# Softplus from ScalarE's table in a four-layer state-space model with a mixture of experts

## The chip, the cores and the metric

The kernel runs on one core of a Trainium2 chip. The metric is the device time of one execution in microseconds (us), the median of some runs. The engines of the core work side by side, each through its own list of instructions in order, and wait for each other on semaphores: TensorE (PE in the profile, PEld its weight loads), VectorE (DVE), ScalarE (ACT), GpSimd (POOL), and the queue of SyncE (SP), which issues most of the DMAs.

## What is computed

4096 tokens (16 sequences of 256) of width 128 go through four layers of a state-space block, then a residual and a layer norm, then a mixture of 8 experts (the best 2 of them per token) with residual and layer norm. Everything is in fp32. The block, cut to what matters here:

```python
def _mamba_block(x, p):
    xn = _rmsnorm(x, p['norm_w'])
    xp, z = jnp.split(xn @ p['Win'], 2, axis=-1)
    xc = silu(conv(xp, p['conv_w'], p['conv_b']))
    dt, Bm, Cm = jnp.split(xc @ p['Wx'], [64, 80], axis=-1)
    delta = jax.nn.softplus(dt @ p['Wdt'] + p['bdt'])
    A = -jnp.exp(p['A_log'])
    # per token t: h = exp(delta_t * A) * h + (delta_t * xc_t) * B_t ;  y_t = h . C_t
    y = (scan(xc, delta, A, Bm, Cm) + xc * p['Dp']) * silu(z)
    return x + y @ p['Wblk']
```

The inner width is 256, the state has 16 entries per channel. softplus(v) is log(1 + exp(v)).

## The kernel before, in words

**Steps and windows.** The tokens are cut into 8 groups of 512 (two sequences); four layers times 8 groups make 32 steps. Every engine's code is written as a function `window(s, ...)` of 16 slots, in which step s is scanned while step s + 1 is prepared and step s - 1 is finished. `windows` calls it for s = -1 (prologue), 0 and 1, then in a hardware loop over pairs for s = 2 to 29, then for 30, 31 and 32. The expert stage behind it has 8 groups in the same form (`group_pairs`: two written out, two turns of a loop over pairs, two written out).

**A scan slot.** A slot scans two units of 32 channels by 4 state entries. ScalarE makes the decays exp(delta * A) of a slot from `d_rep` (L563, two of 510 columns) into a ring of 4; GpSimd and ScalarE make the products du * B (`outer`, L469 and L472, L641), one quarter m of the state for all channels in four slots; TensorE turns them to channels (`to_channels`, L1067); VectorE scans (L829); VectorE and GpSimd multiply by C in turn (`times_c`, L838 and L478); TensorE sums (L1052).

**Preparing step s + 1.** On ScalarE, in order: slot 3 the silus of xc and z (`silus`, L574 and L579), with a table load before and one after; slot 5 the copy of dt, B and C (L587); slot 6 the root of the norm of step s + 2; slots 7 and 8 softplus; slot 10 the copy of B (L617); slot 14 the copies of du turned to tokens (`copy_dut`, L626, into `du_t`). Between them stand the decays and products of every slot. TensorE feeds these through two banks, `pre_ps`: taps, z (`project_z`, L1090, at slot 2), dt (L1108), the turns of B and du (L1145, at slot 11). GpSimd multiplies delta by xc to du at slot 10 (L488). At slot 12 GpSimd's list has `outer` of the next step's first quarter with no product in it, only the waits for `du_t` and B, and behind it the multiplication by C of slot 11.

**Softplus.** It is computed as max(v, 0) + log(1 + exp(-|v|)), the logarithm bounded from above by a short polynomial. ScalarE: Abs and Relu of both 512-column halves out of PSUM with the bias dt (L600, L601), then Exp (L605), Square (L608) and Ln (L610) over all 1024 columns. VectorE, at slot 8: two fused operations and an addition (L860, L864, L868), which give `delta` and release du and the copies of delta. All seven activations have their functions in the table set that the decays use, so no table is loaded for them.

**Queues.** SP issues in order for each window: the rows of C (`c_rep`), in even windows the output weights (`w_out`, after the output projection of the step before), then 16 copies of delta into `d_rep` (L357), which the decays of the next window read. In even windows ScalarE issues the load of the next weights (`w_pre`) right behind the Ln (L654), in odd windows a smaller one at slot 12. Instructions come to the engines by DMA as well (queues named instruction in the profile).

Of the kernel before, what the change touches and what calls it, by code (L numbers as in the profile page):

```python
# [10 lines left out]
ALU = mybir.AluOpType  # L11
# [5 lines left out]
EXPERTS, HID = 8, 512  # L17
# [22 lines left out]
LOG_SCALE = 3.0 ** -0.5  # L40
LOG_BIAS = -0.75 * LOG_SCALE
LOG_ADD = 13.0 / 16.0
LN_ERROR = 2.0 ** -23
# [22 lines left out]
def build_program(nc, xT, x_rows, norm_w, Win, conv_w, conv_b, Wx, Wdt, bdt, A_log, Dp, Wblk, Wout, bout,  # L66
                  gate_w, w1, w2, out):
    ctx = ExitStack()
    with ctx:
# [3 lines left out]
        def sem(name):  # L73
# [13 lines left out]
        sp_e = sb("sp_e", [128, KT, TG])  # L87
        sp_w = sb("sp_w", [128, KT, TG])
        sp_l = sb("sp_l", [128, KT, TG])
        delta = sb("delta", [128, KT, TG])  # L90
        du = sp_l
# [10 lines left out]
        one = sb("one", [128, 1])  # L102
        log_bias = sb("log_bias", [128, 1])
# [7 lines left out]
            sp_l[:, 0, JT * EXPERTS * i:JT * EXPERTS * (i + 1)].rearrange("p (j e) -> p j e", j=JT)  # L111
# [59 lines left out]
        x_in = [sp_e[:, i, :] for i in range(2)]  # L171
        x_fin = sp_w[:, 0, :]
        res1 = sp_w[:, 1, :]
# [41 lines left out]
        dt_used = sem("dt_used")  # L215
# [3 lines left out]
        act_sp = sem("act_sp")  # L219
        sp_ready = sem("sp_ready")  # L220
        dve_sp = sem("dve_sp")
# [54 lines left out]
        def wait(eng, semaphore, value):  # L276

            if isinstance(value, int) and value <= 0:
                return
            eng.wait_ge(semaphore, value)  # L280
# [25 lines left out]
        def has(s, offset):  # L306

            return not isinstance(s, int) or 0 <= s + offset < STEPS

        def group_pairs(eng, stage_fn):  # L310

            for par in (0, 1):
                stage_fn(par, 0, par)
            with eng.Fori(1, GROUPS // 2 - 1) as i:
                for par in (0, 1):
                    stage_fn(2 * i + par, i, par)
            for par in (0, 1):
                stage_fn(GROUPS - 2 + par, GROUPS // 2 - 1, par)
# [5 lines left out]
        def _(sp):  # L324
# [42 lines left out]
            def window(s, i, par):  # L367
                nxt = 1 - par
                if is_last(s):
                    sp.wait_ge(delta_ready, STEPS)  # L370
# [37 lines left out]
            windows(sp, window)  # L408
# [14 lines left out]
            group_pairs(sp, finish)  # L423
# [932 lines left out]
```

## Time and profile before

| | |
|---|---|
| median of 3 runs | 2142.69 us (2141.18 to 2149.81) |
| profiled execution, span | 2143.5 us |
| VectorE busy | 1943.2 us (91%) |
| TensorE busy | 1877.8 us (88%) |
| ScalarE busy | 1683.8 us (79%) |
| GpSimd busy | 1458.1 us (68%) |
| scan loop and its ends | to about 1710 us |
| expert stage | from about 1710 us to the end |

For the profiled execution the profile gives its span, from the first instruction to the last, and no other time; it lies 0.8 us above the median. In the expert stage TensorE is busy without a break and GpSimd has nothing to do, so the shares of the whole span say little of the scan. Times within the span are counted from its start. A row of a timeline has the start, the length, engine, line, operation, what it writes and reads, how many in a row were merged, and in brackets how long the engine stood idle before and for whom.

### The profile page before, as it was taken

To read this page: it belongs to the slowest core of one execution; us is meant where nothing else is said; L and a number is where in the kernel's file an instruction comes from. 1 tells how busy PE (TensorE), PEld (TensorE's weight loads), DVE (VectorE), ACT (ScalarE), POOL (GpSimd) and SP (SyncE) were. 2 spreads that over 40 slices of the span, in tenths; PEclk is the share of its full clock that TensorE was granted. 3 is DMA by queue.
4 is the path that set the end of the run, shared out by engine and by line. 5 is a ranking of instruction groups with operands and counts; after the bars stand their busy time and mean duration, and the time that the engine had idled before them with its cause. 6 is when DMAs were issued, how large, how long until landed. Compare 5 with 4: busy or idle time off the path is not lost.

```text
span 2143.5 us, 34659 instructions
## 1 busy us (share of the span) xinstructions
PE 1877.8 (88%) x10816; PEld 1183.1 (55%) x10816; DVE 1943.2 (91%) x1826; ACT 1683.8 (79%) x3053; POOL 1458.1 (68%) x1364
## 2 busy tenths in 40 slices
PE   4788888888888888888888888888888799999998
PEld 1444444444444444444444445444444499989998
DVE  3799999999999999999999999999999987767775
ACT  4899999899999998989999999999999433333333
POOL 2688888888888888888888988888889600000000
PEclk9899999999999999999999999999999999999999
DMA  7323232323232323232333333332322200000000
GB/s 241 86 64 79 63 78 62 78 62 78 62 79 63 80 65 79 64 79 65 81 78 73 81 76 79 78 78 62 78 62 72 84 1 11 11 12 11 11 6 11
DMA packets 72786, 138.55 MB, mean 65 GB/s; under 512 B 13072, under 2 KB 31120, under 8 KB 68112
## 3 DMA queue, kind: packets, MB, share of 16 engines
q1 hardware_dynamic: 66320, 119.28, 22.7%
q10 hardware_dynamic: 6400, 18.42, 3.7%
q8 instruction: 39, 0.64, 0.1%
q14 instruction: 27, 0.22, 0.0%
HBM read 63.85 MB, written 7.74 MB: 33 GB/s over the span
## 4 chain that ended last, share of the span: by engine, by line
ACT 27%; PE 26%; POOL 26%; issue 13%; DVE 6%; ACTq 1%; SPq 1%; DMA 1%; POOLq 0%; DVEq 0%
POOL scan L478 12%; POOL scan L472 11%; PE y_ps L1291 11%; ACT decay L563 10%; PE dbu_ps L1266 8%; ACT scan L641 6%; DVE scan L829 3%; POOL scan L469 2%; PE dbu_ps L1067 2%; ACT sp_e L600 2%; ACT delta L601 2%; ACT sp_l L610 2%; PE y_ps L1052 2%; ACT sp_e L605 1%; ACT du_t L626 1%
## 5 line engine op out<-in xcount | busy, mean ns | idle before, releaser
L829 DVE TENSOR_TENSOR_SCAN scan<-decay,dbu_ps 128x1024 f32<-128x1024 f32 x512 | 1154.6, 2274 | 29.8 <-PE dbu_ps L1067 21.9
L1067 PE MATMUL dbu_ps<-ident,scan 128*128 128x128 f32 x4096 | 571.6, 286 | 220.7 <-DVE scan L829 195.9
L478 POOL TENSOR_TENSOR scan<-scan,c_rep 128x1024 f32<-128x1024 f32 x255 | 671.8, 2635 | 130.4 <-ACT du_t L626 66.5
L1067 PEld LDWEIGHTS dbu_ps<-ident,scan 128*128 128x128 f32 x4096 | 482.2, 147 | 500.1 <-DVE scan L829 259.3
L563 ACT ACTIVATE decay<-d_rep,a_cur 128x510 f32<-128x510 f32 x1024 | 668.0, 709 | 54.1 <-POOL scan L478 15.7
L472 POOL TENSOR_SCALAR scan<-du_t,b_t 128x256 f32<-128x256 f32 x896 | 594.8, 679 | 0.0
L641 ACT ACTIVATE scan<-du_t,b_t 128x256 f32<-128x256 f32 x1024 | 445.6, 494 | 1.2
L838 DVE TENSOR_TENSOR scan<-scan,c_rep 128x1024 f32<-128x1024 f32 x257 | 331.0, 1288 | 0.0
L766 ACT ACTIVATE decay<-dbu_ps 128x512 f32<-128x512 f32 x256 | 147.9, 597 | 205.2 <-PE dbu_ps L1266 183.1
L1052 PE MATMUL y_ps<-scan,sel 128*32 128x512 f32 x2048 | 299.8, 661 | 0.0
L1080 PE MATMUL pre_ps<-xn,w_pre 128*128 128x512 f32 x512 | 245.5, 603 | 5.2 <-DVE w_pre L818 5.2
L507 POOL TENSOR_TENSOR sp_e<-sp_e,bout_rep 128x512 f32<-128x512 f32 x8 | 11.2, 1399 | 277.1 <-DMA sp_e<-in_x_rows 277.1
L1266 PE MATMUL dbu_ps<-split_all 128*128 128x512 f32 x768 | 191.3, 400 | 5.8 <-DVE split_all L892 3.5
L1002 DVE TENSOR_TENSOR decay<-decay 128x512 f32<-128x512 f32 x256 | 163.6, 686 | 9.2 <-ACT decay L766 8.1
L1266 PEld LDWEIGHTS dbu_ps<-split_all 128*128 128x128 f32 x768 | 141.1, 190 | 35.2 <-issue 7.7
L989 DVE SCALAR_TENSOR_TENSOR xc<-y_ps,cw,xc 128x128 f32<-128x128 f32 x256 | 72.0, 344 | 95.4 <-PE y_ps L1291 95.4
L1080 PEld LDWEIGHTS pre_ps<-xn,w_pre 128*128 128x128 f32 x512 | 87.8, 191 | 97.4 <-issue 90.6
L488 POOL TENSOR_TENSOR sp_l<-delta,xc 128x1024 f32<-128x1024 f32 x32 | 75.2, 2351 | 81.2 <-DVE delta L868 81.2
L1291 PEld LDWEIGHTS y_ps<-w_pre,decay 128*128 128x128 f32 x1024 | 119.1, 192 | 3.6 <-issue 1.1
L1291 PE MATMUL y_ps<-w_pre,decay 128*128 128x128 f32 x1024 | 119.5, 275 | 0.2 <-DVE decay L1002 0.2
L1291 PEld LDWEIGHTS y_ps<-c_rep,decay 128*128 128x128 f32 x1024 | 118.0, 192 | 1.9
L1291 PE MATMUL y_ps<-c_rep,decay 128*128 128x128 f32 x1024 | 118.1, 275 | 0.0
(110 smaller groups left out, 1648.8 us busy)
## 6 DMA issues: line engine op xcount, KB each, us to landing
d_rep<-delta SPq DMA_DIRECT2D x496, 128.0 KB, 2.9
c_rep<-c_rows SPq DMA_DIRECT2D x32, 1024.0 KB
w_pre<-prepared_weights ACTq DMA_DIRECT2D x15, 866.0 KB, 13.0
prepared_weights<-scan SPq DMA_DIRECT2D x3, 1122.0 KB, 12.9
scan<-in_conv_w SPq DMA_DIRECT2D x4, 512.0 KB, 5.0
w_out<-prepared_weights SPq DMA_DIRECT2D x16, 128.0 KB, 12.5
sp_e<-in_x_rows SPq DMA_DIRECT2D x8, 256.0 KB, 3.2
d_rep<-in_w ACTq DMA_DIRECT2D x2, 1024.0 KB, 6.8
```

Source lines behind the costliest of these rows:

```text
L472: nc.gpsimd.tensor_scalar(dst, src, col, 1.0, ALU.mult, ALU.mult).then_inc(dbut_pool, 1)
L478: nc.gpsimd.tensor_tensor(ring[slot % RING], ring[slot % RING], c_rep[par][:, slot // PRS, :].unsqueeze(1).broadcast_to([128, 2, TG]), ALU ...
L563: last = nc.scalar.activation(decay[slot % DEC][:, u, :, 1:], src[:, :, 1:], ACT.Exp, scale=a_cur[:, b, m:m + 1])
L641: nc.scalar.activation(dbu_t[m % 2][:, j, :, q, :], du_t[par][:, j, :].rearrange("p (b c) -> p b c", b=UNITS), ACT.Copy, scale=b_t[par][:, ...
L829: nc.vector.tensor_tensor_scan(ring[slot % RING].rearrange("p u t -> p (u t)"), decay[slot % DEC].rearrange("p u a t -> p (u a t)"), dbu_p ...
L838: nc.vector.tensor_tensor(ring[slot % RING], ring[slot % RING], c_rep[par][:, slot // PRS, :].unsqueeze(1).broadcast_to([128, 2, TG]), ALU ...
L1002: nc.vector.tensor_tensor(hid[e % 2][:, c, :], hid[e % 2][:, c, :], hid[e % 2][:, c, :], ALU.mult).then_inc(h2_ready, 1)
L1052: last = nc.tensor.matmul(y_ps[k][CH * j:CH * j + CH, :], sel[:, :], ring[slot % RING][:, j % 2, :], start=False, stop=m == M - 1, skip_gr ...
L1067: last = nc.tensor.transpose(dbu_ps[slot % 2][:, u, 128 * j:128 * j + 128], dbu_t[m % 2][:, j, b, :, :].rearrange("p q c -> p (q c)"), ide ...
L1080: tap = nc.tensor.matmul(o, w_pre[:, c0:c0 + 128], xn[:, :, k:k + SEQ], start=k == 0, stop=k == KC - 1, skip_group_check=True)
L1266: last = nc.tensor.matmul(dst, left[l], right[r], start=start and n == 0, stop=stop and n == len(passes) - 1)
L1291: last = nc.tensor.matmul(moe_ps[e % 2][:, DM * j:DM * j + DM], hid[e % 2][:, c, 128 * j:128 * j + 128], w2_sb[e][:, c, :], start=c == 0, ...
```

## The change

ScalarE computes softplus with its own function, one activation for each half out of PSUM into `delta`, in slot 7. The function lies in another table set, so a table load stands before the two and one after them, as around the silus. The seven activations and VectorE's three operations are gone, and with them their tiles; `du`, the router's scratch, the input rows and the residual get tiles of their own. `delta_ready` is now given by ScalarE's second half; TensorE's turn of B waits for the first half, the output projection for the second. GpSimd's du moves from slot 10 to slot 9, ahead of the products of that slot. The load of the next weights follows the second table load. The hardware loops are gone: windows and expert groups are all written out.

```diff
-            def softplus_parts(s):
+            def softplus(s):
                 wait(act, du_ready, s)
                 for k in range(KT):
                     act.wait_ge(dt_ready, 2 * s + k + 1)
-                    bias = w_pre[:, W_DB + k:W_DB + k + 1]
-                    bank = pre_ps[1 - k][:, :]
-                    nc.scalar.activation(sp_e[:, k, :], bank, ACT.Abs, bias=bias)
-                    nc.scalar.activation(delta[:, k, :], bank, ACT.Relu, bias=bias).then_inc(dt_used, 1)
-
-            def softplus_logs(s):
-                act.wait_ge(dt_used, 2 * s + 2)
-                nc.scalar.activation(sp_e[:, :, :], sp_e[:, :, :], ACT.Exp, scale=-1.0).then_inc(act_sp, 1)
-                act.wait_ge(act_sp, s + 1)
-                wait(act, dut_mm, 2 * s)
-                nc.scalar.activation(sp_w[:, :, :], sp_e[:, :, :], ACT.Square, scale=LOG_SCALE,
-                                     bias=log_bias[:, :])
-                nc.scalar.activation(sp_l[:, :, :], sp_e[:, :, :], ACT.Ln, bias=one[:, :])\
-                    .then_inc(sp_ready, 1)
+                    nc.scalar.activation(delta[:, k, :], pre_ps[1 - k][:, :], ACT.Softplus,
+                                         bias=w_pre[:, W_DB + k:W_DB + k + 1])\
+                        .then_inc(delta_ready if k == KT - 1 else delta_low, 1)
+                load_exp_and_ln()
...
                     if slot == 7 and has(s, 1):
-                        softplus_parts(s + 1)
-                    if slot == 8 and has(s, 1):
-                        softplus_logs(s + 1)
+                        softplus(s + 1)
                         if par == 0 and has(s, 2):
-                            act.wait_ge(sp_ready, s + 2)
+                            act.wait_ge(delta_ready, s + 2)
...
-                        if slot == 8:
-                            dve.wait_ge(sp_ready, s + 2)
-                            nc.vector.scalar_tensor_tensor(out=sp_w[:, :, :], in0=sp_w[:, :, :], scalar=LOG_ADD,
-                                                           in1=sp_e[:, :, :], op0=ALU.add, op1=ALU.mult)\
-                                .then_inc(dve_sp, 1)
...
-                            nc.vector.tensor_tensor(delta[:, :, :], delta[:, :, :], sp_l[:, :, :], ALU.add)\
-                                .then_inc(delta_ready, 1)
...
-                    if slot == 10 and has(s, 1):
+                    if slot == 9 and has(s, 1):
                         pool.wait_ge(delta_ready, s + 2)
+                        wait(pool, dut_mm, 2 * (s + 1))
                         nc.gpsimd.tensor_tensor(du[:, :, :], delta[:, :, :], xc[nxt][:, :, :], ALU.mult)\
                             .then_inc(du_ready, 1)
...
-        def windows(eng, window):
-
-            window(-1, -1, 1)
-            for s in (0, 1):
-                window(s, 0, s)
-            with eng.Fori(1, PAIRS - 1) as i:
-                for par in (0, 1):
-                    window(2 * i + par, i, par)
-            for s in (STEPS - 2, STEPS - 1):
-                window(s, PAIRS - 1, s % 2)
-            window(STEPS, PAIRS, 0)
+        def windows(window):
+
+            for s in range(-1, STEPS + 1):
+                window(s, s // 2, s % 2)
```

ScalarE, in an even window, slots 7 to 9, before: `decay` is written by the decays, `scan` by the products, `sp_e`, `sp_w` and `sp_l` are softplus's own tiles.

```order
L563 ACTIVATE decay<-d_rep,a_cur 128x2x255 x2
L641 ACTIVATE scan<-du_t,b_t 128x8x32 x3
L600 ACTIVATE sp_e<-pre_ps,w_pre 128x512
L601 ACTIVATE delta<-pre_ps,w_pre 128x512
L600 ACTIVATE sp_e<-pre_ps,w_pre 128x512
L601 ACTIVATE delta<-pre_ps,w_pre 128x512
L563 ACTIVATE decay<-d_rep,a_cur 128x2x255 x2
L605 ACTIVATE sp_e<-sp_e 128x1024
L608 ACTIVATE sp_w<-sp_e,log_bias 128x1024
L610 ACTIVATE sp_l<-sp_e,one 128x1024
L654 DMA w_pre<-prepared_weights 128x1732
L563 ACTIVATE decay<-d_rep,a_cur 128x2x255 x2
```

The same place now:

```order
L539 ACTIVATE decay<-d_rep,a_cur 128x2x255 x2
L607 ACTIVATE scan<-du_t,b_t 128x8x32 x3
L574 ACT_TABLE_LOAD
L574 ACTIVATE delta<-pre_ps,w_pre 128x512 x2
L501 ACT_TABLE_LOAD
L620 DMA w_pre<-prepared_weights 128x1732
L539 ACTIVATE decay<-d_rep,a_cur 128x2x255 x4
```

The whole of softplus, both loads and the issue of the weight load now stand ahead of the decays of slot 8, which were between its two parts; those of slots 8 and 9 follow each other.

GpSimd, slots 8 to 12 of a window that is written out, before: L478 multiplies by C, L469 and L472 are products, L488 is du.

```order
L469 TENSOR_TENSOR scan<-du_t,b_t 128x8x32
L472 TENSOR_SCALAR scan<-du_t,b_t 128x8x32 x3
L478 TENSOR_TENSOR scan<-scan,c_rep 128x1024
L472 TENSOR_SCALAR scan<-du_t,b_t 128x8x32 x2
L488 TENSOR_TENSOR sp_l<-delta,xc 128x1024
L472 TENSOR_SCALAR scan<-du_t,b_t 128x8x32 x2
L478 TENSOR_TENSOR scan<-scan,c_rep 128x1024 x2
```

The same place now:

```order
L446 TENSOR_TENSOR scan<-du_t,b_t 128x8x32
L449 TENSOR_SCALAR scan<-du_t,b_t 128x8x32 x3
L455 TENSOR_TENSOR scan<-scan,c_rep 128x1024
L466 TENSOR_TENSOR du<-delta,xc 128x1024
L449 TENSOR_SCALAR scan<-du_t,b_t 128x8x32 x4
L455 TENSOR_TENSOR scan<-scan,c_rep 128x1024 x2
```

du went ahead of two products; what stands behind slot 10 has the same place.

## Rows read from the trace of the kernel before

**Rows 1.** Busy time by engine, 200 us of the loop (stretch, length, engines, clock, DMA).

```profile
core 0: us, PE busy (x) PEld busy (x) DVE busy (x) ACT busy (x) POOL busy (x), PEclk, DMA share, GB/s
600.00:800.00 200.00, 173.31 (x946) 93.75 (x945) 195.37 (x115) 183.94 (x333) 175.93 (x164) 0.94 0.30 73
```

**Rows 2.** Waits: engine and line, for whom: us in total, times, longest.

```profile
ACT sz L579 <- PE pre_ps L1090: 73.6, 64, 2.4
...
POOL sp_l L488 <- DVE delta L868: 81.2, 32, 8.9
...
POOL scan L478 <- ACT du_t L626: 66.5, 31, 2.5
...
PE dbu_ps L1067 <- POOL scan L472: 20.8, 31, 2.8
...
ACT decay L563 <- DMA d_rep<-delta: 12.7, 6, 5.0
```

**Rows 3.** Timeline of ScalarE, z of an odd window to du_t.

```profile
634.77 0.60 ACT L579 ACTIVATE sz<-pre_ps 128x512 f32 x1 [2.33 <-PE pre_ps L1090]
...
648.37 0.67 ACT L600 ACTIVATE sp_e<-pre_ps,w_pre 128x512 f32<-128x512 f32 x1
...
650.64 1.33 ACT L563 ACTIVATE decay<-d_rep,a_cur 128x510 f32<-128x510 f32 x2
651.87 1.05 ACT L605 ACTIVATE sp_e<-sp_e 128x1024 f32<-128x1024 f32 x1
...
655.05 1.32 ACT L563 ACTIVATE decay<-d_rep,a_cur 128x510 f32<-128x510 f32 x2
...
666.19 1.09 ACT L626 ACTIVATE du_t<-pre_ps 128x512 f32<-128x512 f32 x2
```

**Rows 4.** Timeline of GpSimd from du_t on.

```profile
667.43 2.87 POOL L478 TENSOR_TENSOR scan<-scan,c_rep 128x1024 f32<-128x1024 f32 x1 [1.71 <-ACT du_t L626]
...
676.42 0.93 POOL L472 TENSOR_SCALAR scan<-du_t,b_t 128x256 f32<-128x256 f32 x2
...
677.91 2.35 POOL L472 TENSOR_SCALAR scan<-du_t,b_t 128x256 f32<-128x256 f32 x3
```

**Rows 5.** Timeline of TensorE, the z projections of three windows.

```profile
633.57 1.88 PE L1090 MATMUL pre_ps<-xn,w_pre 128*128 128x512 f32 x4
...
684.75 1.88 PE L1090 MATMUL pre_ps<-xn,w_pre 128*128 128x512 f32 x4
...
736.29 1.88 PE L1090 MATMUL pre_ps<-xn,w_pre 128*128 128x512 f32 x4
```

**Rows 6.** Groups by line: table loads ahead of silu (busy, mean ns; idle).

```profile
L574 ACT ACT_TABLE_LOAD x32 | 41.1, 1283 | 0.6
```

**Rows 7.** Timeline of ScalarE at the silus of the next window.

```profile
680.96 1.28 ACT L574 ACT_TABLE_LOAD   x1
682.26 1.36 ACT L574 ACTIVATE xc<-pre_ps,w_pre 128x512 f32<-128x512 f32 x2
686.02 0.60 ACT L579 ACTIVATE sz<-pre_ps 128x512 f32 x1 [2.40 <-PE pre_ps L1090]
```

**Rows 8.** Timeline of ScalarE behind softplus and a weight load.

```profile
707.02 1.33 ACT L563 ACTIVATE decay<-d_rep,a_cur 128x510 f32<-128x510 f32 x2 [0.70 <-ACT sp_l L610]
```

**Rows 9.** Timeline of VectorE at softplus: its first operation, and the scan behind.

```profile
655.17 1.23 DVE L860 SCALAR_TENSOR_TENSOR sp_w<-sp_w,sp_e 128x1024 f32<-128x1024 f32 x1 [0.73 <-ACT sp_l L610]
...
658.99 2.28 DVE L829 TENSOR_TENSOR_SCAN scan<-decay,dbu_ps 128x1024 f32<-128x1024 f32 x1
```

**Rows 10.** Timelines of the prologue: ScalarE's Abs and VectorE's last addition.

```profile
32.51 0.69 ACT L600 ACTIVATE sp_e<-pre_ps,w_pre 128x512 f32<-128x512 f32 x1 [0.62 <-PE pre_ps L1108]
...
40.78 1.22 DVE L868 TENSOR_TENSOR delta<-delta,sp_l 128x1024 f32<-128x1024 f32 x1
```

**Rows 11.** Timeline of TensorE, z projections of windows 1 and 2.

```profile
120.00 1.88 PE L1090 MATMUL pre_ps<-xn,w_pre 128*128 128x512 f32 x4
...
171.14 1.88 PE L1090 MATMUL pre_ps<-xn,w_pre 128*128 128x512 f32 x4
```

**Rows 12.** Busy time by engine, one group of the expert stage (columns as rows 1).

```profile
1877.74:1933.49 55.75, 53.29 (x374) 48.79 (x373) 38.81 (x106) 20.45 (x39) 1.29 (x1) 1.00 0.04 12
```

More of the change, by code:

```diff
@@ L36 @@
 EPS = 1e-5
[L40 to L43, printed above, removed]
 JT = TG // 128
@@ L170, in build_program @@
         y_lo = [y_parts[:, i, 1, :] for i in range(2)]
-        x_in = [sp_e[:, i, :] for i in range(2)]
-        x_fin = sp_w[:, 0, :]
-        res1 = sp_w[:, 1, :]
+        x_in = [x_in_all[:, i, :] for i in range(2)]
+        x_fin = fin[:, 0, :]
+        res1 = fin[:, 1, :]
         y_ff = [sz[:, 2, i, :] for i in range(2)]
@@ L276, in wait @@
         def wait(eng, semaphore, value):
-            if isinstance(value, int) and value <= 0:
+            if value <= 0:
                 return
@@ L306, in has, with groups @@
         def has(s, offset):
[L308 to L318, printed above, removed]
+            return 0 <= s + offset < STEPS
+        def groups(stage_fn):
+            for g in range(GROUPS):
+                stage_fn(g, g // 2, g % 2)
         block = ctx.enter_context(nc.Block())
@@ L406, in window @@
                             .then_inc(w2_loaded[e // half], 16)
-            windows(sp, window)
+            windows(window)
             out_rows = out.rearrange("a s d -> (a s) d")
@@ L510, in _ @@
             normalise(0)
-            windows(pool, window)
+            windows(window)
             def prepare_next(g, i, par):
@@ L515, in prepare_next @@
                     add_bout(g + 1, i if par == 0 else i + 1, 1 - par)
-            group_pairs(pool, prepare_next)
+            groups(prepare_next)
         @block.scalar
@@ L767, in relu @@
                         .then_inc(relu_ready, 1)
-            windows(act, window)
+            windows(window)
             def experts(g, i, par):
@@ L785, in experts @@
                             route(g + 1)
-            group_pairs(act, experts)
+            groups(experts)
             root_ff(GROUPS - 1, 1)
@@ L822, in scan @@
             def scan(s, slot):
-                if isinstance(s, int) and s == 0 and slot in (0, RING // 2):
+                if s == 0 and slot in (0, RING // 2):
                     dve.wait_ge(made_stored[2 + slot // (RING // 2)], 16)
@@ L1003, in square @@
                                             ALU.mult).then_inc(h2_ready, 1)
-            windows(dve, window)
+            windows(window)
             def experts(g, i, par):
@@ L1032, in experts @@
                 stats_of(g, 1, acc[par])
-            group_pairs(dve, experts)
+            groups(experts)
             norm2(GROUPS - 1, 1, out_done[1], 16 * (GROUPS // 2 - 1))
@@ L1162, in skip @@
                 wait(pe, g_ready, 2 * s - 1 + k)
-                if isinstance(s, int) and s == 0:
+                if s == 0:
                     pe.wait_ge(first_rep, Q)
@@ L1178, in window @@
                         to_channels(s, slot)
-                    if slot < 2 and isinstance(s, int) and s == 0:
+                    if slot < 2 and s == 0:
                         project_conv(1, slot, 0, KC)
@@ L1253, in logits @@
                 wait(pe, router, ROUTER_OPS * g)
-                if isinstance(g, int) and g == 1:
+                if g == 1:
                     pe.wait_ge(x_ready, X0 + STEPS)
@@ L1271, in up @@
                 pe.wait_ge(y_split, 2 * (g + 1))
-                if isinstance(g, int) and g == 0:
+                if g == 0:
                     pe.wait_ge(w_split, 2 * (e + 1))
@@ L1284, in down @@
             def down(g, e):
-                if isinstance(g, int) and g == 0 and e % half == 0:
+                if g == 0 and e % half == 0:
                     pe.wait_ge(w2_loaded[e // half], 16 * half)
@@ L1294, in down @@
                 last.then_inc(down_ready, 1)
-            windows(pe, window)
+            windows(window)
             def experts(g, i, par):
                 for e in range(EXPERTS):
-                    if not (isinstance(g, int) and g == 0 and e < 2):
+                    if not (g == 0 and e < 2):
                         up(g, par, e)
@@ L1311, in experts @@
                 down(g, EXPERTS - 1)
-            group_pairs(pe, experts)
+            groups(experts)
 def is_first(g, e):
-    return isinstance(g, int) and g == 0 and e == 0
+    return g == 0 and e == 0
 def has_group(g, offset):
-    return not isinstance(g, int) or g + offset < GROUPS
+    return g + offset < GROUPS
 NAMES = ["norm_w", "Win", "conv_w", "conv_b", "Wx", "Wdt", "bdt", "A_log", "Dp", "Wblk", "Wout", "bout"]
```

45 lines of the change are left out of this document (14 added, 31 removed).

## Prediction

> **What bounds the kernel now.** I read the busy shares first, then the list of waits, then the timelines of ScalarE, GpSimd and TensorE over two windows of the scan loop, and went round the waits until they closed. A window is one pass of 16 slots, in which one step is scanned and the next one prepared; 32 of them are scanned, one more stands ahead.
>
> In 200 us out of the loop VectorE is busy 195.4, ScalarE 183.9, GpSimd 175.9 and TensorE 173.3 [rows 1]. The eye goes to VectorE. The waits tell another story [rows 2]. ScalarE waits for the z projection twice in every window (64 times, 73.6 us in all), GpSimd waits for du_t in 31 windows, TensorE for GpSimd's products in 31. These three make a ring. One turn of it, at the first of the two windows in [rows 3] to [rows 5]:
> - ScalarE's leg. From the first silu of z (634.77) to the end of the du_t copies (666.19 + 1.09 = 667.28) it works through its list with no gap of over 0.6 us: 32.5 us.
> - GpSimd's leg. It stands at slot 12 until du_t is there, starts at 667.43, and has the products of the next step's first quarter done at 676.42 + 0.93 = 677.35.
> - TensorE's leg. It waited for these products, then goes through transposes and taps in its written order and reaches the z projection at 684.75. ScalarE has by then finished the silus of x and stands; the z silu starts at 686.02 [rows 7].
>
> The z projections start at 633.57, 684.75 and 736.29 [rows 5]: one turn takes 51.18 and 51.54 us, the second in windows where ScalarE also issues a weight load. Each leg ends in an engine that stood waiting for it, so the ring has no slack. What is taken from ScalarE's leg shortens the window by that much; what is taken from VectorE alone does not.
>
> **The change part by part.** All is reckoned against the profiled execution, span 2143.5 us, which is 0.8 over the median of the runs, 2142.69; the same 0.8 comes off at the end.
>
> ScalarE, removed. In the first window the four Abs and Relu run from 648.37 to the next decay at 650.64, 2.27 us, and Exp, Square and Ln from 651.87 to 655.05, 3.18 [rows 3]: 5.45 us, all inside ScalarE's leg. In a window with a weight load ScalarE also stands 0.70 behind Ln, for the semaphore of the Ln and the DMA issue behind it, and loses 0.09 of overlap [rows 8]: 6.24.
>
> ScalarE, added. Two table loads and two activations of 512 columns out of PSUM with a bias column. The load has 32 rows of its own kind, mean 1.283 us [rows 6]; from the start of the load ahead of silu to the start of its first activation are 682.26 - 680.96 = 1.30, and the two silus, same shape, same source, same kind of bias, take 1.36 [rows 7]. The load back is again 1.30. With 0.08 for the overlap that a load does not have with what ran before it: 4.04. No row shows a Softplus. Bounds: 0.57 each as for the Abs and Relu when they follow each other (2.27 for four), and on the other side 1.06 each, which would be Exp, Square and Ln's pace of 1024 columns (3.18 for three) on half the columns. I take the silu's 0.68, since four functions at this size differ by under a fifth; the upper end would cost 0.76 more in each of 31 windows, 24 us.
>
> The weight load's issue then waits for the second softplus, which is over when the load back begins; the issue fits beside that load. So the 0.79 goes. At worst it stays: 12 us.
>
> ScalarE's leg is thus shorter by 1.41, and by 2.20 with a weight load. Softplus is in windows 0 to 30, 15 of them with a load: 16 x 1.41 + 15 x 2.20 = 55.6 us.
>
> Here a rule speaks against the change. The Trainium skill ("ScalarE: Activation LUTs", What ACT_TABLE_LOAD costs) gives 2.66 us for every switch to another set, a load of 1.28 and a drain of 1.38. The trace agrees with the load alone; no gap of that size stands ahead of or behind it [rows 6, 7]. By the page's figure the two loads would cost 2.76 more in a window and the sum would come to about 2160.
>
> VectorE. Its three operations take 655.17 to 658.99, 3.82 us, after 0.73 of idle time [rows 9]. Nothing is saved by this in the ring: VectorE's 195.4 of 200 is 50.1 in a window and becomes 46.3, below the 49.6 that ScalarE's leg now allows. What is late next on VectorE is the decay of slot 8, which stands behind the whole softplus on ScalarE: I expect a wait of one to two microseconds there. It is covered: 49.6 - 46.3 leaves VectorE 3.3 us in a window.
>
> GpSimd. du needs delta, which now comes straight from ScalarE, by the old clock at 648.5 + 1.30 + 1.36 = 651.1, not from VectorE's last addition, over near 659. GpSimd stood 81.2 us for it in 32 windows [rows 2], 2.5 each; it reached the place at 656.5, and slot 9, two products sooner, at about 654.7. So that wait goes. The two products of slot 9 come behind du, but the whole quarter is wanted at slot 12 and its last product stands behind the same work as before. No gain: GpSimd stands at slot 12 for du_t as before (66.5 us in 31 windows), only longer.
>
> d_rep copies (SP). They start on delta, and ScalarE waited 12.7 us for them, 6 times in all [rows 2]. In every other window they stand behind w_out on SP's queue, which waits for TensorE's output projection; there they start little sooner, and ScalarE wants them 2.2 sooner. I count 1 us, bounds 0 and 12.7.
>
> Prologue. Nothing hides softplus there. Before: ScalarE starts Abs at 32.51 after 0.62 idle, delta is ready at 40.78 + 1.22 = 42.00 [rows 10]. After: the load starts in that idle time, delta is ready near 31.9 + 1.30 + 1.36 = 34.6. That is 7.4; I count 6, since the copies that follow now meet the stores of the weights. Bounds 3 and 7.4.
>
> Written out. Windows 0 and 1 are straight code already: the turn from one to the next takes 171.14 - 120.00 = 51.14, against 51.18 in the loop [rows 11, 5]. I take 0.1 for each of 28 windows, 3 us, bounds 0 and 11 (51.54 against 51.14). In the expert stage TensorE bounds, and one group of tokens takes 55.75 with only 53.29 of TensorE work [rows 12]; its end is where the loop of groups turns back. The gap of 2.5 goes, bounds 0 and 2.5.
>
> Sum: 55.6 + 1 + 6 + 3 + 2.5 = 68.1. 2143.5 - 68.1 = 2075.4, less 0.8: 2074.6, rounded 2075 us.
>
> **The rivals.**
> - GpSimd's leg changes. A product that takes 0.47 when it runs free (two in 0.93) takes about 0.94 longer when VectorE multiplies by C beside it (three in 2.35 [rows 4]). Now one or two such collisions fall in this leg; VectorE's phase against GpSimd moves by some 1.6 us. One more in every window is 31 x 0.94 = 29 us: 2104. One fewer: 2046. Either sign is open.
> - VectorE is the bound after all, and its 3.82 + 0.73 come off each window: 31 x 4.55 = 141 us in place of 55.6, 1989. For it: 98% busy. Against it: the ring of waits, and VectorE's own idle time, of which 0.73 a window is a wait for ScalarE's Ln [rows 9].
> - Slower: each added table load holds ScalarE as long again as it runs, waiting for the engine to run empty. Place: between the decays of slots 7 and 8, in the ring. Price from the load's own row: 62 loads x 1.283 = 80 us, 2155. It decides from 68.1 / 62 = 1.1 us a load. Against it: 64 loads of the same engine between the same kinds of activations show no such gap. The page's drain, named above, is this case, at 2160.
> - No change: straight code has to be brought in where the loop stood still. If an engine in the ring stood 2.2 us in a window for that, the gain is gone: 2143. Against it: the 51.14 of the straight window.
>
> **How the numbers follow.** Forecast 55%, own range 2055 to 2095 (the activation's length and the smaller bounds). A longer GpSimd leg 16%, a shorter one 14%, VectorE 4%, slower loads 6%, no change 5%. The range 2040 to 2112 holds the first, most of the second and third. A measurement of this kernel can tell 0.5%, 10.7 us, from no change: faster than 2132 is 0.88, within 0.05, slower 0.07.
>
> **What would show it.** Table loads of 1.28 with no gap, two per window more than now; softplus near 0.68; z projections 49.8 and 49.3 us apart; ScalarE still standing about 2.3 us for z and GpSimd for du_t, with no wait for delta; VectorE under 95% busy, with its largest wait at slot 8 for ScalarE's decay. The forecast is wrong if z no longer waits (another ring took over), if a gap stands at the loads, or if GpSimd's stretch from du_t to its last product moves from 9.9 us.

## The result

The changed kernel takes 2154.1 us (median of 12 runs, 2142.2 to 2163.5), the kernel before 2143.0 beside it: a ratio of 1.0049, 95% interval 1.0033 to 1.0066. It is 0.5% slower, where 2075 us was forecast.

### The profile page after: what moved, and what is told of

The parts are those of the page before. It is cut to its first block and busy times, and to the rows that moved or that the text cites. A ratio compares the mean times of both kernels' runs of the same rounds, so it can differ in the third digit from the quotient of the medians.

```text
span 2155.7 us, 30569 instructions
## 1 busy us (share of the span) xinstructions
PE 1863.9 (86%) x10816; PEld 1164.5 (54%) x10816; DVE 1809.7 (84%) x1728; ACT 1632.2 (76%) x2957; POOL 1418.2 (66%) x1364
## 3 DMA queue, kind: packets, MB, share of 16 engines
q1 hardware_dynamic: 66320, 119.28, 27.7%
## 5 line engine op out<-in xcount | busy, mean ns | idle before, releaser
L455 POOL TENSOR_TENSOR scan<-scan,c_rep 128x1024 f32<-128x1024 f32 x255 | 692.3, 2715 | 209.3 <-ACT du_t L592 102.7
L539 ACT ACTIVATE decay<-d_rep,a_cur 128x510 f32<-128x510 f32 x1024 | 665.6, 710 | 164.3 <-DMA d_rep<-delta 90.8
L1016 PEld LDWEIGHTS dbu_ps<-ident,scan 128*128 128x128 f32 x4096 | 467.7, 144 | 484.8 <-DVE scan L791 232.2
L1016 PE MATMUL dbu_ps<-ident,scan 128*128 128x128 f32 x4096 | 563.4, 282 | 183.3 <-DVE scan L791 118.7
L449 POOL TENSOR_SCALAR scan<-du_t,b_t 128x256 f32<-128x256 f32 x896 | 529.9, 608 | 0.0
L800 DVE TENSOR_TENSOR scan<-scan,c_rep 128x1024 f32<-128x1024 f32 x257 | 316.4, 1231 | 2.3 <-DMA c_rep<-c_rows 2.3
L1029 PE MATMUL pre_ps<-xn,w_pre 128*128 128x512 f32 x512 | 275.7, 667 | 24.0 <-DMA w_pre<-prepared_weights 18.8
L1001 PE MATMUL y_ps<-scan,sel 128*32 128x512 f32 x2048 | 274.9, 609 | 0.0
L485 POOL TENSOR_TENSOR x_in<-x_in,bout_rep 128x512 f32<-128x512 f32 x8 | 11.2, 1400 | 274.7 <-DMA x_in<-in_x_rows 274.7
L1029 PEld LDWEIGHTS pre_ps<-xn,w_pre 128*128 128x128 f32 x512 | 97.2, 210 | 130.9 <-issue 102.0
L446 POOL TENSOR_TENSOR scan<-du_t,b_t 128x256 f32<-128x256 f32 x128 | 81.4, 636 | 71.7 <-PE dbu_ps L1016 69.6
## 6 DMA issues: line engine op xcount, KB each, us to landing
w_pre<-prepared_weights ACTq DMA_DIRECT2D x15, 866.0 KB, 18.5
```

The source lines that it names most:

```text
L449: nc.gpsimd.tensor_scalar(dst, src, col, 1.0, ALU.mult, ALU.mult).then_inc(dbut_pool, 1)
L455: nc.gpsimd.tensor_tensor(ring[slot % RING], ring[slot % RING], c_rep[par][:, slot // PRS, :].unsqueeze(1).broadcast_to([128, 2, TG]), ALU ...
L539: last = nc.scalar.activation(decay[slot % DEC][:, u, :, 1:], src[:, :, 1:], ACT.Exp, scale=a_cur[:, b, m:m + 1])
L800: nc.vector.tensor_tensor(ring[slot % RING], ring[slot % RING], c_rep[par][:, slot // PRS, :].unsqueeze(1).broadcast_to([128, 2, TG]), ALU ...
L1001: last = nc.tensor.matmul(y_ps[k][CH * j:CH * j + CH, :], sel[:, :], ring[slot % RING][:, j % 2, :], start=False, stop=m == M - 1, skip_gr ...
L1016: last = nc.tensor.transpose(dbu_ps[slot % 2][:, u, 128 * j:128 * j + 128], dbu_t[m % 2][:, j, b, :, :].rearrange("p q c -> p (q c)"), ide ...
```

## The profile after

Busy time in the same 200 us of the loop (columns as in [rows 1]):

```profile
600.00:800.00 200.00, 171.14 (x932) 91.60 (x925) 175.86 (x100) 175.15 (x319) 169.00 (x164) 0.97 0.40 73
```

VectorE fell from 195.37 to 175.86, 88% of the stretch (under 95% was forecast), but every other engine fell too: all of them wait more. For whom they wait, the list of waits tells (columns as [rows 2]):

```profile
POOL scan L455 <- ACT du_t L592: 102.7, 31, 3.4
...
ACT decay L539 <- DMA d_rep<-delta: 90.8, 23, 12.5
...
ACT decay L539 <- issue: 55.5, 15, 5.3
...
PE dbu_ps L1016 <- POOL scan L449: 42.7, 18, 2.8
ACT sz L555 <- PE pre_ps L1039: 39.9, 64, 2.2
```

ScalarE's wait for the copies of delta went from 12.7 to 90.8 us, with 55.5 more in 15 windows where the profile names no releaser but the line is the same. Both kinds go when the loads of C go (a run below), so both are put down to the copies. Its wait for z fell from 73.6 to 39.9: the ring is partly open now. Of GpSimd's wait for delta (81.2) 1.3 is left.

ScalarE, from z of one window to du_t, and on to z of the next:

```profile
634.30 0.60 ACT L555 ACTIVATE sz<-pre_ps 128x512 f32<-128x512 f32 x1 [0.64 <-PE pre_ps L1039]
...
647.82 1.28 ACT L574 ACT_TABLE_LOAD   x1
649.12 1.27 ACT L574 ACTIVATE delta<-pre_ps,w_pre 128x512 f32<-128x512 f32 x2
650.40 1.28 ACT L501 ACT_TABLE_LOAD   x1
651.70 2.56 ACT L539 ACTIVATE decay<-d_rep,a_cur 128x510 f32<-128x510 f32 x4
...
664.04 1.07 ACT L592 ACTIVATE du_t<-pre_ps 128x512 f32<-128x512 f32 x2
...
672.25 1.33 ACT L539 ACTIVATE decay<-d_rep,a_cur 128x510 f32<-128x510 f32 x2 [3.21 <-issue]
...
685.99 0.60 ACT L555 ACTIVATE sz<-pre_ps 128x512 f32<-128x512 f32 x1 [0.64 <-PE pre_ps L1039]
```

Softplus and both table loads take 651.70 - 647.82 = 3.88 us with no gap. Behind du_t ScalarE then stands 3.21 for the copies. GpSimd, VectorE and TensorE in the same window:

```profile
665.25 2.36 POOL L455 TENSOR_TENSOR scan<-scan,c_rep 128x1024 f32<-128x1024 f32 x1 [3.32 <-ACT du_t L592]
...
673.78 1.89 POOL L449 TENSOR_SCALAR scan<-du_t,b_t 128x256 f32<-128x256 f32 x2
```

```profile
674.06 1.26 DVE L800 TENSOR_TENSOR scan<-scan,c_rep 128x1024 f32<-128x1024 f32 x1
```

```profile
675.73 1.88 PE L1016 MATMUL dbu_ps<-ident,scan 128*128 128x128 f32 x8 [2.61 <-POOL scan L449]
677.40 2.82 PE L1029 MATMUL pre_ps<-xn,w_pre 128*128 128x512 f32 x4
...
684.83 1.98 PE L1039 MATMUL pre_ps<-xn,w_pre 128*128 128x512 f32 x4
```

The last two products take 1.89, not 0.93 [rows 4]; VectorE multiplies by C beside them. TensorE, which has stood 2.61 us, then takes 1.88 for the 8 transposes and 2.82 for the taps. At the same place before it had stood 0.56 and took 1.09 and 1.88, at a granted clock (third from last in the lower row) of 1.00:

```profile
677.50 1.09 PE L1067 MATMUL dbu_ps<-ident,scan 128*128 128x128 f32 x8 [0.56 <-POOL scan L472]
678.42 1.88 PE L1080 MATMUL pre_ps<-xn,w_pre 128*128 128x512 f32 x4
```

```profile
677.50:679.50 2.00, 2.00 (x11) 1.49 (x12) 2.00 (x3) 2.00 (x5) 2.00 (x3) 1.00 0.00 0
```

The table has the ring's three legs, before [rows 3 to 5, 7], after, and in a run below that mends the two losses (its rows stand there):

| leg, us | before | after | with TensorE's clock kept, no loads of C |
|---|---|---|---|
| ScalarE, z to end of du_t | 32.51 | 30.81 | 30.79 |
| GpSimd, to end of products | 10.07 | 10.56 | 10.57 |
| TensorE, to the next z on ScalarE | 8.67 | 10.32 | 8.38 |
| turn | 51.25 | 51.69 | 49.74 |

ScalarE's leg lost 1.70; 1.41 was forecast for a window of this kind, without a weight load. TensorE's leg grew by 1.65, GpSimd's by 0.5. Over all 30 turns from the second z projection to the last the mean is 52.13, before 51.50.

Queue SP, the load of the rows of C and the copies of delta, after and then before (start, time over which they are issued):

```profile
642.83 0.57 SPq L359 DMA_DIRECT2D c_rep<-c_rows  x1
650.46 12.94 SPq L335 DMA_DIRECT2D d_rep<-delta  x16
```

```profile
643.43 0.57 SPq L382 DMA_DIRECT2D c_rep<-c_rows  x1
659.15 10.24 SPq L357 DMA_DIRECT2D d_rep<-delta  x16
```

This is a window without `w_out`: the load of C stands where it stood, the copies begin 8.7 us sooner. What that does to the DMA engines (next to last column their busy share, last GB/s), after and before:

```profile
652.00:658.00 6.00, 4.83 (x25) 2.59 (x22) 4.89 (x3) 6.00 (x13) 6.00 (x6) 1.00 1.04 138
658.00:664.00 6.00, 4.45 (x38) 3.17 (x37) 6.00 (x4) 6.00 (x12) 3.92 (x3) 1.00 1.10 147
```

```profile
652.00:658.00 6.00, 4.78 (x26) 2.31 (x18) 5.21 (x5) 5.97 (x9) 4.75 (x4) 1.00 0.25 82
...
664.00:670.00 6.00, 5.25 (x40) 3.08 (x32) 6.00 (x4) 5.97 (x12) 4.29 (x2) 0.85 0.91 203
```

Before, C runs alone at a share of 0.25, then the copies alone at 0.91 and 203 GB/s. After, both together take over 1.0 and move 138 to 147. In the windows with `w_out` the copies begin only 2.9 us sooner (707.50 for 710.44). But there the load of the next weights, issued behind the second table load, starts 4.4 us sooner and runs into the load of C. First its issue before, then after, with ScalarE's wait at the start of the window behind:

```profile
706.53 0.37 ACTq L654 DMA_DIRECT2D w_pre<-prepared_weights  x1
```

```profile
702.09 0.34 ACTq L620 DMA_DIRECT2D w_pre<-prepared_weights  x1
...
726.06 1.33 ACT L539 ACTIVATE decay<-d_rep,a_cur 128x510 f32<-128x510 f32 x2 [5.47 <-DMA d_rep<-delta]
```

The weights land in 18.9 us in this window, before in 10.8, and the copies come in among them. Over the whole run the profile's DMA issues say the same: a copy lands in 6.3 us, not 2.9; the weights in 18.5, not 13.0. The bytes are equal, 119.28 MB.

## The experiments

All ratios are to the kernel before on the same chip, with 95% intervals. "Turn" is the time between two z projections.

**Copies behind the load of C**, to undo the overlap by a wait:

```diff
+                    sp.wait_ge(c_loaded[nxt], 16 * ((s + 1) // 2 + 1))
                     replicate(s + 1, nxt)
```

> The changed kernel, with one wait more on SP: the copies of delta start only when the rows of C of the same step have landed (steps after the first). Theory A, collision: in the changed kernel the copies start about 8 us sooner and meet the load of C's rows on the DMA engines (16 us at a quarter of them), so that each takes 6.3 us to land where it took 2.9, and ScalarE waits 4 to 5 us for them at the start of each window. With the wait the landing falls back to about 3 us, ScalarE's wait to 1 to 3 us, and the time to about 2100. Theory B, written-out code: SP and the queues serve copies more slowly without the loop; landing stays at 6 us, the copies start later still, and the time rises above 2200. Theory C, a deadline only: the copies take what they took, ScalarE merely asks sooner; then they come 9 us later than now and the time rises by about 8 us a window, to 2350.

2164.1 us, 1.0080 (1.0055 to 1.0106): the landings are theory A's, short again (2.4 us), the time is that of no theory. ScalarE waits 136.0 us for the copies in 48 places: they start at 673.1 in a window whose du_t is over at 676.9. Load and copies in a row are too long for the shorter window.

**No loads of C** but for the first two steps:

```diff
-                if has(s, 1):
+                if has(s, 1) and s < 1:
                     sp.wait_ge(c_stored, 16 * (s + 2))
...
```

Later steps multiply by the rows of C of the first two.

> The changed kernel without the load of C's rows after the first two steps (all later steps multiply by the rows of steps 0 and 1). Theory A, collision with the load of C: copies of delta land in about 3 us, ScalarE's wait at the window's start goes, one turn of the ring is 49.3 to 49.8 us as predicted, time 2065 to 2090. Theory B, written-out code: landing stays at 6 us, time stays near 2154. If the weight load in even windows is the partner in the collision, odd windows become fast and even ones stay at 52 us: about 2115.

2127.4 us, 0.9929 (0.9907 to 0.9952): faster than theory B, slower than theory A. The copies land in 2.5 us and the weights in 4.4, the waits for the copies are gone but for two at the start, in both kinds of windows, and from the fourth on every turn is 51.2, not 49.7. So the loads of C, by way of the copies, cost 27 us, and a second loss is laid bare. TensorE there:

```profile
665.22 1.97 PE L1016 MATMUL dbu_ps<-ident,scan 128*128 128x128 f32 x8 [2.60 <-POOL scan L449]
666.98 2.52 PE L1029 MATMUL pre_ps<-xn,w_pre 128*128 128x512 f32 x4
...
673.95 1.88 PE L1039 MATMUL pre_ps<-xn,w_pre 128*128 128x512 f32 x4
```

From the products to z are 8.73 us; before, 7.25 (677.50 to 684.75). Third from last in this row of the stretch is the granted clock, 0.50, the lower of its two levels, 1.2 GHz:

```profile
665.00:667.00 2.00, 1.78 (x9) 1.78 (x10) 0.00 (x0) 2.00 (x5) 2.00 (x5) 0.50 0.00 0
```

**The kernel before, only written out straight:**

```diff
-            with eng.Fori(1, PAIRS - 1) as i:
-                for par in (0, 1):
-                    window(2 * i + par, i, par)
+            for s in range(-1, STEPS + 1):
+                window(s, s // 2, s % 2)
...
```

> The kernel before, with windows and expert groups written out and nothing else changed. Theory A: the loop was worth little, 3 us in the scan and 2.5 in the expert stage as predicted, landing of the copies stays at 2.9 us: 2137. Theory B, written-out code makes the copies slow: landing rises toward 6 us and the time above 2160.

2132.8 us, 0.9942 (0.9926 to 0.9959): 11 us, where the forecast had 3 + 2.5. The copies land in 2.9 us as before, so written-out code is not what makes them slow. The rest of the change thus cost 21 us.

**C behind the copies** on SP's queue:

```diff
-                if has(s, 1):
-                    sp.wait_ge(c_stored, 16 * (s + 2))
...
                     replicate(s + 1, nxt)
+                if has(s, 1):
+                    sp.wait_ge(c_stored, 16 * (s + 2))
...
```

> The changed kernel with SP's order turned: the copies of delta first, the load of C's rows behind them. Theory A, collision: copies land in about 3 us and early, ScalarE does not wait for them; the rows of C come about 17 us after the last copy, shortly before VectorE's first multiplication by C wants them: 2075 to 2100, with a new small wait there if they are late. Theory B, written-out code: landing stays at 6 us, gain small, 2130 to 2154.

2126.7 us, 0.9927 (0.9904 to 0.9949), between the two theories. The copies land in 2.5 us, as theory A has it, but C is late now:

```profile
POOL scan L455 <- DMA c_rep<-c_rows: 67.8, 16, 17.8
DVE scan L800 <- DMA c_rep<-c_rows: 44.1, 16, 11.3
```

From the second turn on TensorE's stretch from the products to z takes 7.25 to 7.27 in some turns and 8.67 to 8.96 in the others, nothing between; the shortest turns, 48.7 to 49.8, all have the short one.

**TensorE's clock kept** in the run without loads of C, by work for nothing where it stood:

```diff
+                wait(pe, scan_done, SLOTS * s + slot - 1)
+                if slot == 0 and s > 0:
+                    for f in range(FILL):
+                        nc.tensor.transpose(dbu_ps[0][:, f % 2, 128 * (f // 2 % JT):128 * (f // 2 % JT) + 128],
+                                            ident[:, :], ident[:, :])
                 if p == 0:
                     pe.wait_ge(dbut_pool, POOL_OUTER * (M * s + m + 1))
                     pe.wait_ge(dbut_act, ACT_OUTER * (M * s + m + 1))
-                wait(pe, scan_done, SLOTS * s + slot - 1)
...
```

FILL is 16.

> The changed kernel with C loaded for the first two steps alone (as in the run that took the C loads out, 2127.4 us, whose turns were all 51.2), and on TensorE 16 turns of the identity into the bank of slot 0, in the time in which it stood 2.6 us for GpSimd's last products of the first quarter. The output of the later layers isn't the reference's, since C is stale. Theory A (the ring's TensorE leg runs at half clock behind that standing time): the granted clock there goes from 0.50 to about 1.0, the transposes of slot 0 from 1.97 to 1.05, the taps from 2.52 to 1.88; the turn loses 1.3 to 1.6 us and comes to 49.6 to 49.9; the time is 2127 - 31 x 1.45 = 2082, 2075 to 2090. Theory B (the turn of 51.2 is set by GpSimd or by the taps' place, the clock only shows beside it): clock 1.0 too, but turns of 51.0 to 51.2, time 2120 to 2128. Theory C (the extra turns are in the way): over 2130.

2085.3 us, 0.9731 (0.9712 to 0.9749). Every turn but the first two is 49.7 to 49.8.

```profile
652.20 1.91 PE L1013 MATMUL dbu_ps<-ident 128*128 128x128 f32 x16
654.98 1.09 PE L1021 MATMUL dbu_ps<-ident,scan 128*128 128x128 f32 x8 [0.87 <-POOL scan L450]
655.90 1.88 PE L1034 MATMUL pre_ps<-xn,w_pre 128*128 128x512 f32 x4
...
662.24 1.88 PE L1044 MATMUL pre_ps<-xn,w_pre 128*128 128x512 f32 x4
```

```profile
654.90:659.00 4.10, 4.03 (x22) 2.77 (x23) 2.59 (x2) 4.08 (x8) 4.10 (x6) 1.00 0.00 0
```

The stretch is 7.26 again, the granted clock 1.00. Sixteen useless transposes save 42 us: TensorE's clock was the second loss. ScalarE and GpSimd of this run, the rows behind the table above:

```profile
613.56 0.60 ACT L556 ACTIVATE sz<-pre_ps 128x512 f32<-128x512 f32 x1 [2.19 <-PE pre_ps L1044]
...
643.29 1.06 ACT L593 ACTIVATE du_t<-pre_ps 128x512 f32<-128x512 f32 x2
663.30 0.60 ACT L556 ACTIVATE sz<-pre_ps 128x512 f32<-128x512 f32 x1 [2.19 <-PE pre_ps L1044]
```

```profile
653.03 1.89 POOL L450 TENSOR_SCALAR scan<-du_t,b_t 128x256 f32<-128x256 f32 x2
```

**The same 16 transposes in the changed kernel**, loads of C as they were:

> The changed kernel as it is, rows of C ahead of the copies of delta, with the 16 turns of the identity on TensorE ahead of slot 0 that kept its clock. Theory A (the two losses, the copies of delta and the clock, lie one behind the other in the ring and add up): clock near 1.0, 2154 - 31 x 1.4 = 2111, 2105 to 2118. Theory B (the copies of delta alone set the turn, as ScalarE waits for them wherever the ring stands): 2148 to 2160.

2150.1 us, 1.0035 (1.0015 to 1.0055): theory B. While the copies are late the clock gives nothing that can be told (the changed kernel is at 1.0049); ScalarE's wait for them is 91.2 us, in the changed kernel 90.8. The two losses lie beside each other, not in a row: mending the clock shows only once the copies are in time.

**GpSimd's wait for du_t a slot later**, behind a multiplication by C, with C behind the copies:

```diff
-                    if m == M and has(s, 1):
+                    if m == M and has(s, 1) and slot > SLOTS - PRS:
                         outer(s + 1, nxt, 0, POOL_FIRST[slot % PRS], POOL_FIRST[slot % PRS + 1])
```

> The changed kernel with the rows of C loaded behind the copies of delta (2126.7 us), and GpSimd's empty outer of slot 12 left out, so that it waits for du_t at slot 13, behind the multiplication by C of slot 11 (2.36 us). Theory A (the ring ScalarE, GpSimd, TensorE still sets the turn): GpSimd's wait for du_t falls from 3.3 to about 1 us a window, its products are there 2.36 sooner, the turn goes from 51.2 to 48.8, less if TensorE, which stands less, keeps its clock; time 2127 - 31 x 2.36 = 2054, 2015 to 2060. Theory B (with the softplus gone another chain sets the turn, for instance VectorE with its waits for ScalarE's decays and TensorE): turns of 50.5 or more, 2105 to 2130.

2107.6 us, 0.9846 (0.9825 to 0.9867): the time is theory B's, but where C is in time the turn falls as theory A has it. From the fourth on every other turn is 47.5 to 47.7; those between are 48.9 to 55.4, since C is late (78.8 us of waits on GpSimd, 81.1 on VectorE).

**ScalarE's copies of du a slot sooner**, with C behind the copies:

```diff
-                    if slot == 14 and has(s, 1):
+                    if slot == 13 and has(s, 1):
                         copy_dut(s + 1, nxt)
```

> The changed kernel with the rows of C loaded behind the copies of delta (2126.7 us), and ScalarE's copies of du to tokens one slot sooner, at slot 13, ahead of the two decays of slot 14 (1.32 us). Theory A (ring): GpSimd starts 1.3 sooner, the turn comes to 49.9, time 2127 - 31 x 1.3 = 2087, down to 2050 if TensorE stands less and keeps its clock. Theory B (another chain sets the turn): 2120 to 2130. Theory C (the copies meet TensorE's turn of du, which ends only about 0.3 us before): half of the gain, 2105 to 2112.

2102.7 us, 0.9815 (0.9790 to 0.9840), between A and C in time, with the same pattern: 47.6 to 47.9, and 49 to 55 where C is late.

**Both moves, and C behind the copies as four loads**, each with a semaphore that is waited for at its first use:

```diff
+                    for m in range(M):
+                        sp.dma_start(c_rep[nxt][:, m, :],
+                                     bass.AP(tensor=rows.tensor, offset=rows.offset + m * TG,
+                                             ap=[[M * TG, Q], [0, CH], [1, TG]]))\
+                            .then_inc(c_loaded[nxt][m], 16)
...
```

> A version meant to be better: the changed kernel with the rows of C loaded behind the copies of delta, as four loads of one quarter with a semaphore each; the copies of du at slot 13; GpSimd's wait for du_t at slot 13. Theory A (ring): 1.3 and 2.36 come off the turn of 51.2, and TensorE's clock with it, until VectorE with its 46.3 us of work and 1.8 of waits is next: turns of 47.5 to 48.2, time 2127 - 31 x 3.3 = 2025, 2010 to 2035. Theory B (another chain): over 2090.

2009.4 us, 0.9376 (0.9361 to 0.9392), just under theory A's range; turns of 47.4 to 47.6 but the first and one of 48.1.

```profile
600.00:800.00 200.00, 178.11 (x1032) 97.25 (x1032) 192.91 (x110) 191.11 (x349) 186.77 (x175) 1.00 0.32 84
```

VectorE is at 192.9 of 200 and stands only 1.8 us a window, ahead of the scan whose decays come behind softplus on ScalarE: it is the next bound.

**du back at slot 10**, with C behind the copies:

```diff
-                    if slot == 9 and has(s, 1):
+                    if slot == 10 and has(s, 1):
                         pool.wait_ge(delta_ready, s + 2)
```

> One part undone: the changed kernel with the rows of C loaded behind the copies of delta (2126.7 us), and GpSimd's du back at slot 10, behind the two products of slot 9. Theory A (du has slack: it was over at 651.35 in the run before this one, TensorE took it at 655.04 after a wait for ScalarE's x): no change that can be told, 2118 to 2136. Theory B (du sooner carried part of the gain, its two products of 1.9 us come ahead of it on the ring): 2126.7 + 31 x 1.9 = 2186. Theory C (products sooner for the next quarter, phase against VectorE): faster by up to 31 x 0.94, 2098.

2113.5 us, 0.9853 (0.9827 to 0.9878), slightly better than with du at slot 9 and in no theory's range: TensorE's stretch takes 7.26 in 16 of 30 turns here, in 11 there. That this is the whole difference isn't shown; du sooner gained nothing.

**Both moves in the kernel before, written out**, softplus as it was, edits as above:

> The kernel before written out straight (2132.8 us), with softplus as before, and the two moves that the better version has: ScalarE's copies of du at slot 13, GpSimd's wait for them at slot 13. It tells whether that version owes its time to the moves alone. Theory A (VectorE, with softplus's 3.82 us still on it, has 50.1 us of work in a window and is the next bound): turns of 50.2 to 51.0, 2105 to 2132. Theory B (the moves are the whole gain): turns near 48, 2030 to 2045.

2129.1 us, 0.9926 (0.9907 to 0.9945), turns of 51.1: theory A by its time. VectorE is the bound:

```profile
600.00:800.00 200.00, 176.31 (x955) 98.66 (x954) 196.44 (x115) 185.04 (x338) 179.23 (x165) 0.93 0.31 74
```

So the table's softplus is worth some 2129 - 2009 = 120 us, once nothing else holds the ring. The two runs differ in C's loads and du's slot as well; what these give in this kernel was not run.

**Both losses mended, nothing else:** C behind the copies as four loads, and the 16 transposes, edits as above.

> Both losses of the changed kernel mended with nothing left out: the rows of C behind the copies of delta, as four loads with a semaphore each, and the 16 turns of the identity that keep TensorE's clock; the softplus, du, ScalarE's copies and GpSimd's waits as in the changed kernel. Theory A (the two losses are the whole of what the forecast missed): flat turns of 49.7 to 49.8 as in the run without loads of C, first z at 54 instead of 65, 2085 - 11 = 2074, 2068 to 2086. Theory B (the loads of C still cost something behind the copies): turns that alternate or are over 50.2, 2090 to 2110.

2072.6 us, 0.9668 (0.9652 to 0.9684), turns of 49.7 to 49.8 but three. The forecast was 2075.

**C over all DMA engines**, at its old place ahead of the copies:

```diff
-                    sp.dma_start(merged(c_rep[nxt]),
-                                 bass.AP(tensor=rows.tensor, offset=rows.offset,
-                                         ap=[[M * TG, Q], [0, CH], [1, M * TG]]))\
+                    for q in range(Q):
+                        sp.dma_start(merged(c_rep[nxt])[CH * q:CH * q + CH, :],
+                                     bass.AP(tensor=rows.tensor, offset=rows.offset + q * M * TG,
+                                             ap=[[0, CH], [1, M * TG]]))\
```

> The changed kernel with the load of the rows of C as four loads, one for each group of 32 partitions, at its old place ahead of the copies of delta; bytes and order as before. As one load it took some 16 us at a DMA share of 0.25, which is four engines of 16. Theory A (it runs on four engines since its outermost count is 4, and the copies of delta wait for their shares on these four; a load with 32 outermost goes over all 16): the load is over in 5 to 8 us, before the copies begin; they land in 2.4 to 2.8 us in place of 6.3, ScalarE waits no more for them in most windows, turns of 51.2 as in the run without loads; 2112 to 2130. Theory B (the source in DRAM or the bytes are the bound, however many engines): share and length of the load as before, landings near 6, 2150 to 2165.

2117.6 us, 0.9886 (0.9864 to 0.9908); landings 2.5, every turn from the third on 51.2: theory A.

```profile
624.70:630.70 6.00, 6.00 (x39) 3.11 (x32) 6.00 (x4) 5.95 (x12) 4.92 (x4) 1.00 0.77 175
```

The load, issued at 624.68, takes a share of 0.77 at 175 GB/s, not 0.25. That it is now four loads is not the reason: the four loads of the run just above, each with an outermost count of 4, still run at 0.26 once the copies are over:

```profile
632.00:638.00 6.00, 4.78 (x33) 2.68 (x36) 6.00 (x5) 5.89 (x13) 5.45 (x6) 1.00 0.26 75
```

The Trainium skill ("DMA: Bandwidth & Descriptors", Rules for kernel authors) says that an outermost dimension smaller than 16 confines a DMA to at most that many engines; the load's was 4. The trace agrees with its share of 0.25 before, and 0.77 with 32 outermost.

**The same with the two moves:**

> The same with ScalarE's copies of du at slot 13 and GpSimd's wait for them at slot 13: the better version with another cure for the copies of delta. Theory A (any cure of the copies gives the same turn, set by VectorE): flat turns of 47.6; 2005 to 2025, later by up to 11 if the prologue still waits for its copies. Theory B (the loads now come in the way of something else, the copies or the weights): over 2040.

2011.4 us, 0.9388 (0.9366 to 0.9410), turns of 47.6. Either cure of the copies does.

## Why the prediction was wrong

The ring, ScalarE's leg and the table loads were right: the leg lost 1.7 us in windows without a weight load and 2.4 in those with one (medians of 32.45 and 33.19 became 30.81), where 1.41 and 2.20 were forecast, and no table load has a gap.

```profile
L574 ACT ACT_TABLE_LOAD x32 | 41.1, 1283 | 0.6
L574 ACT ACTIVATE delta<-pre_ps,w_pre 128x512 f32<-128x512 f32 x64 | 40.5, 684 | 0.4
```

Softplus takes 0.684, the silu's 0.68. The rival of slow loads is out: that its 2155 stands beside the measured 2154 is chance. The drain of 1.38 that the Trainium skill gives ("ScalarE: Activation LUTs", What ACT_TABLE_LOAD costs) does not show here: the idle time ahead of these 32 loads is 0.6 us in all. VectorE's wait at slot 8 is 1.8 at the most, inside the one to two forecast.

- The step that failed first: "there they start little sooner, and ScalarE wants them 2.2 sooner. I count 1 us, bounds 0 and 12.7", on the copies of delta. It asked when the copies start, and in the windows with w_out alone, not what runs on the DMA engines then. In the other windows they start 8.7 us sooner and fall into the load of C, which before was just over as they began. In those with w_out they do start little sooner, 2.9 us, but the weight load, whose earlier issue the forecast priced on ScalarE alone, starts 4.4 us sooner, runs into the load of C, and the copies come late all the same. The term was counted as a gain of 1 us; without the loads of C the kernel is 27 us faster.
- The second: TensorE's leg was taken as fixed ("goes through transposes and taps in its written order"). Its length held only at full clock. Before, TensorE stands longest while VectorE does softplus, and pays for that right behind (a granted clock of 0.50 from 661 to 663), off the ring, as ScalarE goes on to du_t without a gap [rows 3]:

```profile
661.33 1.97 PE L1067 MATMUL dbu_ps<-ident,scan 128*128 128x128 f32 x8 [4.55 <-DVE scan L829]
```

  With VectorE's operations gone it stands 2.6 us right ahead of the leg and runs part of the leg at half clock: 8.73 us for 7.26, with no loads of C in the way. Cost there: 42 us. No rival had it.
- The rival on GpSimd's leg was right in kind: the last two products meet VectorE's multiplication by C and take 0.96 longer, but the leg's first multiplication takes 2.36 for 2.87, and the leg is 0.5 longer, not 0.94.
- "Written out" was too small, 5.5 for 11: the mean turn of the kernel before falls from 51.50 to 51.23 by it, 8 us over 30 turns where 3 were forecast. The stage of the experts gave about what was forecast, 3.0 for 2.5: a group takes 52.74 and TensorE is busy in all of it, against [rows 12].

```profile
1893.26:1946.00 52.74, 52.74 (x374) 48.83 (x373) 38.69 (x106) 20.40 (x40) 1.29 (x1) 1.00 0.04 11
```

- The term for the prologue was too large: 6 for 2.3 (first z of step 1 at 65.25, before 67.58). Delta is there at 34.1 (34.6 forecast), but its copies are not:

```profile
58.25 1.33 ACT L539 ACTIVATE decay<-d_rep,a_cur 128x510 f32<-128x510 f32 x2 [12.53 <-DMA d_rep<-delta]
```

One reading was off without weight: GpSimd reached du's place at 656.75 (659.16 - 2.41), not 656.5.

With both losses mended the time is 2072.6. Of the 81 us from the changed kernel to this one, 27 and 42 are the two losses as measured above, and 10 are the prologue (first z of step 1 at 64.86 in the run with the clock kept, at 54.59 here). The time is 2 us from the forecast partly by luck: the turns gave (51.50 - 49.70) x 30 = 54 us, where the ring and the straight windows were to give 59.6, the prologue 13 for 6 (first z of step 1 at 54.59), the experts' stage 3 for 2.5. Left open is why the clock falls behind a stand of 2.6 us in some turns and not in others of the same run.

## What to carry to other kernels

When a change makes one link ready sooner, list every transfer that it triggers and what is on the DMA engines at that moment; the broadcast load with an outermost count of 4 ran for some 14 us at a share of 0.25 here, time enough to be run into. A leg of TensorE has two lengths: where an edit takes idle time off one place, find the place where TensorE will stand next, and whether the ring passes there. An edit that pays nothing may have freed an engine: here VectorE's 3.8 us a window were worth some 120 us as soon as the copies were in time and two waits had moved by a slot.

## What the runs showed that I had not expected

- Useless transposes in a gap made the run without loads of C 42 us faster, by TensorE's clock; with the copies still late they gave nothing.
- The same 1 MB is loaded at a share of 0.25 or 0.77 by the outermost count: four loads with a count of 4 stay at 0.26. At a share of 0.25 its overlap with the copies raised their landing from 2.9 to 6.3 us, and both together moved fewer GB/s (138 to 147) than the copies alone (203).
- The version with both moves and either cure takes 2009 to 2011 us, 6.1 to 6.2% less than the kernel before.
